# First layer's experts walked by token halves, each half's norm chain put between other work, and that layer's weight rounding moved to ScalarE

## The reference

```python
x = x + tanh(g_xattn[0]) * L0_xattn(layernorm(x), ctx, ctx, Wu, Wv)
x = x + tanh(g_ffn[0])   * L0_ffn(layernorm(x), gate_w, wg, wu, wd, swg, swu, swd)
x = x + tanh(g_xattn[1]) * L1_xattn(layernorm(x), ctx, ctx, mask, Wq, bq)      # 16 heads of 8
x = x + tanh(g_ffn[1])   * L1_ffn(layernorm(x), ln_g, ln_b, router_w, ...)     # 8 experts, a second layernorm inside
```

## Time and profile before

| | us |
|---|---|
| times of three runs | 791.43, 788.05, 790.73 |
| their median | 790.73 |
| span of the profiled execution, first to last instruction | 791.2 |
| TensorE busy in it | 700.5 (89%) |
| VectorE, ScalarE, GpSimd busy | 553.0, 367.5, 209.9 |
| mean granted TensorE clock | 0.922 |

### The profile page before, as it was taken

One profiled execution on the slowest core, in us unless ns is written; L12 is line 12 of the kernel. 1 busy time (PEld: TensorE's weight loads), 2 busy tenths in 40 slices (PEclk: granted clock), 3 DMA queues, 4 the chain that ended last, 5 costly groups with the idle time before them and its releaser, 6 DMA issues.

```text
span 791.2 us, 10027 instructions
## 1 busy us (share of the span) xinstructions
PE 700.5 (89%) x3468; PEld 547.8 (69%) x3475; DVE 553.0 (70%) x1242; ACT 367.5 (46%) x647; POOL 209.9 (27%) x193
## 2 busy tenths in 40 slices
PE   5989997999898998797999797993759999789997
PEld 2779983889666766675777586771546888567775
DVE  4688766788578585656667735769874554588996
ACT  2334442434435737455275464721214442486673
POOL 5113107322132041124424311143002220214431
PEclk9589997999799999999999989986879999799999
DMA  5102003000001010202010200030000000001000
GB/s 134 39 27 58 2 4 114 31 1 1 1 14 67 3 38 1 68 0 80 14 68 14 66 1 0 1 97 0 1 0 1 1 1 1 27 27 28 1 1 27
DMA packets 27361, 20.97 MB, mean 27 GB/s; under 512 B 5409, under 2 KB 22571, under 8 KB 27311
## 3 DMA queue, kind: packets, MB, share of 16 engines
q1 hardware_dynamic: 26591, 20.29, 8.7%
q10 hardware_dynamic: 720, 0.04, 0.1%
HBM read 19.80 MB, written 0.52 MB: 26 GB/s over the span
## 4 chain that ended last, share of the span: by engine, by line
PE 70%; DVE 17%; issue 4%; ACT 4%; POOL 3%; DMA 1%; ACTq 0%; DVEq 0%; POOLq 0%
PE PS L1366 61%; PE PS L1563 4%; DVE H2l L1082 2%; PE PS L1448 2%; POOL WL L607 2%; ACT H1h L752 1%; DVE SN L1038 1%; PE PS L1499 1%; ACT G L750 1%; DVE WH L936 1%; DVE XN L910 1%; PE PS L1386 1%; DMA GW<-in_L_gate_T 1%; DVE ST L891 1%; POOL RSTD L617 1%
## 5 line engine op out<-in xcount | busy, mean ns | idle before, releaser
L607 POOL TENSOR_TENSOR WL<-RAW,WH 128x512 fp32r<-128x512 f32 (+2 forms) x76 | 95.4, 1272 | 186.9 <-DVE WH L936 186.9
L1082 DVE TENSOR_TENSOR H2l<-G,H2h 128x512 fp32r<-128x512 f32 x104 | 84.0, 822 | 59.7 <-ACT H2h L752 58.7
L1082 DVE TENSOR_TENSOR H1l<-G,H1h 128x512 fp32r<-128x512 f32 x80 | 63.3, 800 | 28.9 <-ACT H1h L752 28.1
L1366 PE MATMUL PS<-H1h,WH 128*128 128x512 f32 x146 | 60.9, 417 | 8.0 <-DVE H1l L1082 8.0
L750 ACT ACTIVATE G<-PS,UB 128x512 f32<-128x512 f32 x64 | 44.8, 700 | 42.4 <-PE PS L1366 38.1
L1366 PE MATMUL PS<-XTh,WH 128*128 128x512 f32 x128 | 55.3, 432 | 9.8 <-POOL WL L607 5.3
L600 POOL TENSOR_TENSOR RSTD<-VE,MHALF 128x4 f32<-128x4 f32 x18 | 19.3, 1072 | 166.5 <-DVE VE L900 166.5
L1366 PEld LDWEIGHTS PS<-V,ATT 77*128 77x128 f32 x512 | 62.5, 192 | 0.6
L625 POOL TENSOR_TENSOR XT<-XT,YW 128x512 f32<-128x512 f32 x24 | 34.8, 1448 | 106.0 <-DVE YW L1017 106.0
L769 ACT ACTIVATE ATT<-ATT 128x308 f32<-128x308 f32 x64 | 29.4, 460 | 71.3 <-DVE ATT L1152 71.0
L1366 PE MATMUL PS<-V,ATT 77*128 77x9 f32 x512 | 61.3, 247 | 0.0
(11 more groups left out here) (242 smaller groups left out, 1677.8 us busy)
## 6 DMA issues: line engine op xcount, KB each, us to landing
RAW<-in_L_ffn_spec_W SPq DMA_DIRECT2D x4, 1024.0 KB, 5.6
RAW<-in_L_ffn_w SPq DMA_DIRECT2D x16, 256.0 KB, 3.0
RAW<-in_L_ffn_up_W SPq DMA_DIRECT2D x8, 256.0 KB, 2.7
RAW<-in_L_ffn_down_W SPq DMA_DIRECT2D x8, 256.0 KB, 3.6
RAW<-in_L_ffn_spec1a_W SPq DMA_DIRECT2D x2, 512.0 KB, 4.3
RAW<-in_L_ffn_spec1b_W SPq DMA_DIRECT2D x2, 512.0 KB, 5.2
RAW<-in_L_ffn_wg SPq DMA_DIRECT2D x4, 176.0 KB, 2.7
RAW<-in_L_ffn_wu SPq DMA_DIRECT2D x4, 176.0 KB, 2.7
```

Source lines behind the costliest of these rows:

```text
L607: g.tensor_tensor(lo, RAW[0:r["rows"], r["raw"] + s["c0"]:r["raw"] + s["c1"]], hi.bitcast(fp32), ALU.subtract).then_inc(lo_done, 1)
L1082: v.tensor_tensor(lo, full, hi.bitcast(fp32), ALU.subtract).then_inc(split_done, 1)
L1366: return t_.matmul(o, l, r, start=start, stop=stop)
```

## The change

Six things are changed, all in layers 0 and 1 but for the last two.

1. Order of layer 0's mixture: (0,0), (0,1), then units 1 to 4 for half 0, then units 1 to 4 for half 1. The first half of `y` is thus finished in step 7 of 12. The strips of units 1 to 4 stand in steps 0 to 3.
2. `high_part` of layer 0's woven strips is done by ScalarE (an `activation` Copy); VectorE keeps it for layers 1 and 3 and for unit 0.
3. The first half's chain (copy of y, turn back, sum, statistics, scaling, turn, query product) stands between pieces of steps 7 to 10, in bank 4. The second half's chain stands in iterations 1 to 12 of layer 1's attention, in bank 5. The 16 idle products are gone.
4. The six high parts of layer 1's first unit are made by VectorE in iterations 10 to 15 of the attention. GpSimd builds the keys of the first two batches as soon as the last `turn0` is split, then does `rstd(5)`, three more keys, the six low parts, and the rest.
5. The turn of the first half for layer 1's mixture moves into the attention's last iterations. The second half's scaling, second statistics and second scaling stand between `up(0,0)` pieces, and two `spec0` products stand before `second`.
6. To free bank 5, transposed groups go to two banks (3 + g % 2) in place of three, in both attentions (layers 1 and 3). `QT`, `SUB`, `PB` and `U0T` get other places; `second` uses bank 5.

```diff
-    x = [(p, h) for p in range(E0P) for h in range(2)]
+    x = [(0, 0), (0, 1)] + [(p, h) for h in range(2) for p in range(1, E0P)]
...
-        more = strips(n // 2 + 1) if n % 2 == 0 and n // 2 + 1 < E0P else []
+        more = strips(n + 1) if n + 1 < E0P else []
...
+        elif n == E0P + 2:
+            order[0] += weave(a, b, c) + chain("y_copy")
+        elif n == E0P + 3:
+            u = weave(a, b, c)
+            order[0] += u[:3] + chain("y_back") + u[3:6] + chain("y_sum") + u[6:8] + chain("y_stats") + u[8:]
+        elif n == E0P + 4:
+            u = weave(a, b, c)
+            order[0] += u[:4] + chain("y_scale") + u[4:8] + chain("x_turn", "x_copy") + u[8:]
+        elif n == E0P + 5:
+            u = weave(a, b, c)
+            order[0] += u[:2] + chain("q_up", "q_copy") + u[2:]
...
-    o += up(0, 0) + second
+    u, s = up(0, 0), group("spec0", 1, 0, 0, TH)
+    o += u[0:1] + chain("late_scale") + u[1:2] + chain("late_stats") + u[2:4] + chain("late_norm") + s[0:2] + second
...
# GpSimd
             pool.wait_ge(ct_ready, 2)
-            rstd(4, 5)
+            rstd(4)
+            pool.wait_ge(split_done, LAST0["hid"])
             head_keys(1, CT, range(2))
+            rstd(5)
+            head_keys(1, CT, range(2, TH + 1))
             prepare(1)
-            head_keys(1, CT, range(2, B - 1))
+            head_keys(1, CT, range(TH + 1, B - 1))
...
# ScalarE
+            def high_part(s_):
+                r = s_["area"]
+                if s_["strip"] == r["first"]:
+                    act.wait_ge(loaded[r["n"]], 16 * len(area_loads(r)))
+                hi, _ = weights(r, s_["c0"], s_["c1"])
+                copy(hi, RAW[0:r["rows"], r["raw"] + s_["c0"]:r["raw"] + s_["c1"]]).then_inc(hi_done, 1)
...
+                    if not first and i == 8:
+                        turned(2, halves=(1,), bank=PS[5])
+                    if not first and i == 10:
+                        queries(1, PS[5])
+                    if not first and i == B * NG + 1:
+                        turned(3, split=True, affine=True, halves=(0,), bank=PS[5])
...
# VectorE
+            def second_half_normed(i):
+                if i == 2:
+                    y0_summed(1, PS[5])
+                elif i == 3:
+                    moments(1, X)
+                elif i == 4:
+                    variances(2, 1)
+                elif i == 6:
+                    scaled(2, 1, X, XN)
+                elif 10 <= i < 10 + len(BEFORE[1]):
+                    high_part(BEFORE[1][i - 10])
...
-            norm(2, X, XN, summed(0))
-            prepare(1)
             attention(0, 1)
+            low_of_xt(1, (0,))
             stats(3, 1, X)
-            low_of_xt(1, (0,))
-            scaled(3, 1, X, XN)
-            dve.wait_ge(xn_ready, TH * (NORM_STEP[3, 1] + 1))
-            stats(4, 1, XN)
-            scaled(4, 1, XN, XM)
-            now(stream_plus_norm(1))
             mixture(1, 1)
...
# TensorE
-                    if g - g0 >= 3:
-                        pe.wait_ge(*copied_out(g - 3))
+                    if g - g0 >= 2:
+                        pe.wait_ge(*copied_out(g - 2))
...
+            def second_half(i):
+                if i == 1:
+                    y0_back(1, PS[5])
+                elif i == 9:
+                    turn(2, *normed(2, XN), halves=(1,), bank=PS[5])
+                elif i == 12:
+                    queries(1, PS[5])
+                elif i == B * NG + 2:
+                    turn(3, *normed(4, XM), halves=(0,), bank=PS[5])
...
-            pe.wait_ge(split_done, LAST0["hid"])
-            turn_back(0)
-            keep_clock(16)
-            turn(2, *normed(2, XN))
-            pe.wait_ge(in_small, SMALL_IN)
-            for i in range(2):
-                pe.wait_ge(xt_ready, 4 + i + 1)
-                mm(PS[i][:, :], WQ1[:, :], XT[:, i * HALF:(i + 1) * HALF]).then_inc(q_full, 1)
             pe.wait_ge(v1_ready, 1)
-            pe.wait_ge(q_ready, 2)
             attention(0, MB1)
-            pe.wait_ge(o_done, B - 1)
-            turn(3, *normed(4, XM), halves=(0,))
             mixture(1, 1, 2)
```

More of the change, by code:

```diff
@@ L701, in mixture @@
                     kind = s_["kind"]
-                    if kind in ("split", "quantise", "down", "down0", "spec0", "spec1b", "weigh"):
+                    if kind in ("split", "quantise", "down", "down0", "spec0", "spec1b", "weigh") or kind in HELD:
+                        if kind == "y_copy":
+                            y0_out(0)
+                        elif kind == "x_copy":
+                            turned(2, halves=(0,), bank=PS[4])
+                        elif kind == "q_copy":
+                            queries(0, PS[4])
+                        elif kind == "split" and layer == 0:
+                            high_part(s_)
                         continue
@@ L708, in mixture @@
                     if kind == "second":
-                        turned(3 if layer == 1 else 7, split=True, affine=layer == 1, halves=(1,))
+                        turned(3 if layer == 1 else 7, split=True, affine=layer == 1, halves=(1,), bank=PS[5])
                         continue
@@ L804, in _ @@
             mixture(0, 0)
[L805 to L813 removed]
+            y0_out(1)
             attention(0, float(DK) ** -0.5)
[L816 removed]
             mixture(1, 1)
@@ L1378, in keep_clock, with turn @@
                     mm(bank[:, :], identb[:, :], MB1[:, 0:HALF])
-            def turn(k, src, ready, halves=range(2)):
+            def turn(k, src, ready, halves=range(2), bank=None):
                 for h in halves:
+                    full = PS[6 + h] if bank is None else bank
                     for t in range(TH):
@@ L1385, in turn, with y0_back, queries @@
                         ready(i)
-                        last = t_.transpose(PS[6 + h][:, t * S:(t + 1) * S], src(i), ident[:, :])
+                        last = t_.transpose(full[:, t * S:(t + 1) * S], src(i), ident[:, :])
                     last.then_inc(xnt_full, 1)
+            def y0_back(h, bank):
+                pe.wait_ge(y0_copied, h + 1)
+                for t in range(TH):
+                    at = h * HALF + t * S
+                    last = t_.transpose(bank[:, t * D:(t + 1) * D], XT[:, at:at + S], ident[:, :])
+                last.then_inc(y_turned, 1)
+            def queries(h, bank):
+                pe.wait_ge(in_small, SMALL_IN)
+                pe.wait_ge(xt_ready, 4 + h + 1)
+                mm(bank[:, :], WQ1[:, :], XT[:, h * HALF:(h + 1) * HALF]).then_inc(q_full, 1)
             def normed(n, buf):
@@ L1411, in mixture @@
                     kind = s["kind"]
-                    if kind in ("split", "quantise", "route", "weigh"):
+                    if kind in ("split", "quantise", "route", "weigh") or kind in HELD:
+                        if kind == "y_back":
+                            y0_back(0, PS[4])
+                        elif kind == "x_turn":
+                            turn(2, *normed(2, XN), halves=(0,), bank=PS[4])
+                        elif kind == "q_up":
+                            queries(0, PS[4])
                         continue
@@ L1580, in attention @@
                 for i in range(B * NG + VALUE_LAG):
+                    if not first:
+                        second_half(i)
                     if i < B * NG:
```

92 lines of the change are left out of this document (58 added, 34 removed).

## The result

The changed kernel takes 810.02 us (median of four runs, 803.14 to 815.81) and the kernel before, run beside it on the same chip, 791.08 (788.05 to 793.03). The ratio is 1.0201, with a 95% interval of 1.0146 to 1.0255; it leaves out the slowest run of the changed kernel, which lies over 1.5% above its fastest. The kernel is slower clear of noise, but whether by more than 2% is not settled. The forecast was 777.1, in a range of 771 to 784: wrong in sign. The profiled execution of the changed kernel is the slowest of its four (815.81 us, span 814.1, clock 0.886); the others have mean clocks of 0.894, 0.896 and 0.905 where before has 0.922. So all four ran longer at the low level; where the level fell in the three that were not profiled is not known.

A forecast was written before the change was run, and what follows sets the result against it. The prediction took TensorE, busy 89% of the span, as the bound. Its terms -2.9 + 1.7 - 15.4 + 1.5 + 3.0 - 1.5 = -13.6 took the 791.2 us span to 777.6, so a median of 777.1, range 771 to 784.

The forecast's parts named there:

- Part 1: Layer 0's mixture: strip casts moved from VectorE to ScalarE shorten a TensorE wait; -2.9 us, bounds 2.0 and 3.5.
- Part 2: Layer 0's mixture: the first half's norm chain adds TensorE work there; +1.7 us, bounds +1.4 and +3.
- Part 3: Between layer 0's mixture and layer 1's attention: the gap of 15.7 us becomes 0.3; -15.4 us.
- rival (c): The gap ahead of layer 1's attention does not close, first keys or queries late; 783 to 786 us, chance 0.06.
- Part 4: Layer 1's attention: the second half's chain adds +1.5 us of TensorE work and +3.0 us of stalls.
- rival (a): No stalls in layer 1's attention, and layer 1's mixture starts at the high clock; 772 us, chance 0.17.
- My rule of one held operation per GpSimd instruction: Layer 1's attention: each running GpSimd instruction holds one SBUF-to-SBUF VectorE operation until it ends; used for the 3.0 us of stalls.
- The 4 that the prediction set beside its 3.0: Layer 1's attention: stalls of 4 us if VectorE operations with two SBUF inputs are held too.
- rival (b): Layer 1's attention: GpSimd's low parts hold VectorE, TensorE waits 7 us or more, clock falls once; 783 us, chance 0.11.
- The last sentence of the prediction: A fall of the granted clock in the attention would upset the whole; no size or chance given.
- Part 5: Start of layer 1's mixture: the first half's turned input arrives earlier, logits end earlier; -1.5 us, bounds -3 and +0.5.

The follow-up runs named there:

- before_casts_on_act: Kernel before, with only layer 0's woven high-part casts moved to ScalarE, mixture order unchanged; 788.45 us, ratio 0.9979.
- after_late_burst: Changed kernel plus 24 idle 512-column products in a row at iteration 24 of layer 1's attention; 794.61 us, ratio 1.0012.
- casts_on_act: Changed kernel with layer 1's six first-unit casts on ScalarE in iterations 4 to 9, ScalarE's query copy one iteration later; 816.28 us, ratio 1.0327.
- two_fillers: Changed kernel plus two idle 512-column products in each of iterations 16 to 31 of layer 1's attention; 781.8 us, ratio 0.9891.
- after_no_idle_2: Changed kernel with turn, query copy, bias rows and fourth key build reordered, two idle 256-column products in each of iterations 30 to 33; 783.01 us, ratio 0.9913.
- after_steady_fillers: Same order as after_no_idle_2, but one idle 512-column product in each of iterations 5 to 9 and 16 to 33 instead; 779.84 us, ratio 0.9857.
- one_burst: Changed kernel plus 24 idle 512-column products in a row at iteration 17 of layer 1's attention; 784.39 us, ratio 0.9924.
- before_vector_late_burst: Kernel before plus five idle VectorE additions in each of iterations 12, 16, 20 and 48 idle 256-column products at 24, layer 1's attention; 817.39 us, ratio 1.032.

## Why the prediction was wrong, step by step

**Part 1** (-2.9): right in kind, -1.7 measured. That is below my bound of 2.0, but its interval (-3.2 to -0.1) holds most of my range, the -2.9 too, so the size is not settled. **Part 2** (+1.7): the mixture's last product ends at 113.54 in the changed kernel, at 112.7 in before_casts_on_act, so the first half's chain costs about 0.85; that is rough, since executions of the kernel before and its variants reach this place up to 1.8 us apart. I forecast 114.6 for that end: 1.1 better. **Part 3** (-15.4): right; the gap is 0.32 us, 0.3 forecast, and rival (c) is out. The first six iterations take 8.7 us (113.86 to 122.58) and not 9.8.

**Part 4** (+1.5 and +3.0): the microseconds are right. Turn and query product cost what I said (the query half 0.94 for 0.9). At the high level (after_late_burst up to its fall) TensorE waits 0.2 at iteration 9, 0.26 at 13, 0.24 at 16 and 3.25 at 20, some 3.9 for my 3.0; rival (a) is out. I had put 0.8 near 20, "where the late key build meets the third bias row", and 0.9 near 16; in fact two builds held two operations in one row at 20. So the sum came out near by luck: its first three terms, 2.2 together, came to 0.7, and its last, 0.8, to 3.25. My rule of one held operation per GpSimd instruction stands in the rows shown here. The Trainium skill, "SBUF — State Buffer", section "SBUF: two separate sides", also lists operations with two SBUF inputs, and the addition to the stream in casts_on_act (0.98 us where 0.29 is normal) agrees. The 4 that the prediction set beside its 3.0 by that rule is close to the 3.9 by luck: the operations held at 20 are a scaling and a cast, not of the two-input kind.

**The step that failed** is the price of a fall of the clock inside the attention: the sum has no term for it, and rival (b) puts it at 2 us: "TensorE waits 7 us or more and the clock falls once: 777.1 + 4 + 2". Waits of 7 us were not needed: 0.26 to 4.2 us stood beside the falls. And the fall costs 36 to 39 us: the 111.4 us from the first scores to layer 1's mixture, against the 79.0 of two_fillers less its 6.9 of products, with up to 3.3 for the waits that these covered. I took the 2 from falls like the one ahead of the attention, which filler or dense products end. I never asked whether the stage in which the fall would come can end it. Its rows could have made me ask: of the 1.98 us of an iteration some 1.25 are transposes and products of nine columns (in the kernel before, 0.81 from 140.51 on and 0.43 from 142.06 on), and no row of mine showed the clock return in such iterations. The last sentence of the prediction named the danger and gave it no chance and no price. The Trainium skill, "TensorE: Matmul & The Clock Gate", section "HAM oscillation — how this bites in real kernels", tells of a clock that is lost in each wait and won back after it. The trace of the changed kernel differs: the level is lost once and, over 88 us of which TensorE was busy 86.8, not won back before the next stage. In after_no_idle_2 it was lost behind a wait and won back 10 us later.

**Part 5** (-1.5): from the first product of layer 1's mixture to the end of the logits and two `spec0` groups it takes 17.8 us before (202.92 to 220.69), 14.7 in the changed kernel (225.26 to 239.92) and 14.0 in after_steady_fillers; and the hole ahead is 1.22 for 2.60. That is over my bound of -3. From there to the end the changed kernel takes 3.7 us more than the kernel before, and after_steady_fillers 2.1 more (572.6 for 570.5). A wait of 1.25 us for `H1l` at 216.60, which the kernel before has not, is part of it; the rest is within what executions differ by there.

**Without the fall** the changed kernel can only be bounded. one_burst, whose clock falls in the tail alone, has a span of 783.0, of which 5.2 are the burst: 777.8. two_fillers, which keeps the level in the tail too, has 778.9, of which 16 times two products at 0.22 are 6.9: 772.0. To either come up to 3.3 us for the waits that the products covered: an estimate of 772 to 781. The forecast of 777.6 for the span lies inside. It was a good sum for a kernel that the chip does not run. One slip of it changes nothing: the lower bounds of its parts add up to 772, not to the 770 that it names.

**What stays open.** Why the fall comes at iteration 14 in the changed kernel and, behind the same instructions, not in one_burst, two_fillers or after_late_burst; and why 0.63 and 0.66 us are survived where 0.55 is not. That a short wait causes a fall is not shown: it may stand beside it by chance. That VectorE was late is shown for the falls at iteration 20, not for the one at 14, whose wait was for ScalarE. A long wait (3.1 to 4.2 us, five kernels) tipped the level each time. The runs of the changed kernel spread from 803 to 816. A fall at iteration 20 and not at 14 would leave six iterations at the high level, an estimate of 6 x 1.87 = 11 us less than the 814.1 us of the profiled execution: 803, beside 801.4 for the span of the fastest. But only one was profiled.

## What to carry to other kernels

Before weighing a wait of TensorE by its microseconds, ask whether the rows show the clock coming back inside the stage around it. If they don't, a fall there can cost as much again as all that remains of the stage at the high clock, and one idle product per iteration, at 0.2 us each, was cheap insurance here. Moving a serial chain into such a stage needs its other engine's list laid out against GpSimd's, instruction by instruction: two long GpSimd operations beside one row of small VectorE ones make the wait. And a hole that is closed can have been harmless where it was, ahead of work that restores the clock.

## What the runs showed of the hardware

The steady iterations mostly kept the level they had: 1.98 us each at the high one, for the 52.9 us on end of the earlier trace rows, and 3.85 at the low one, with TensorE shown busy 50.00 of 50.00 us inside a stretch of 88. One return inside the attention was seen without idle products, at 139.00 in after_no_idle_2. A burst of idle products ended the low level: it began at 196.40 in before_vector_late_burst and the level was high at 198.25. VectorE's held operations end within 0.3 us of the GpSimd instruction beside them, whatever their own size: 16 elements 1.84 us, a row of one partition 2.45. And the fall in the tail of the attention (184.25 in one_burst, 193.5 to 201.5 in variants of the kernel before) came with TensorE idle for less than 0.1 us of the 12 us ahead of it.
